# Scoring the next image's first unit ahead of the weighted groups in the middle steps of a vision-tower kernel

## The reference, cut to what matters

```
h  = tokens(x)                              # (16, 256, 192)
q, k, v = split(layernorm(h) @ W_attn + b)  # 12 heads of 16
s  = where(causal, q @ k.T / 4, -inf)       # (16, 12, 256, 256)
h += softmax(s) @ v @ W_proj + b_proj
h += tree_ffn(layernorm(h))
```

## Time and profile before

| | |
|---|---|
| median of 3 runs | 331.52 us (331.21 to 337.34) |
| profiled execution | 332.06 us |
| its span, first to last instruction | 330.3 us |
| PE busy | 267.7 us, 81% |
| VectorE busy | 224.9 us, 68% |
| ScalarE busy | 193.8 us, 59% |
| GpSimd busy | 186.3 us, 56% |
| mean granted TensorE clock | 0.946 of full speed |
| DMA queue of SP and ACT | 23.69 MB in 23,176 packets |

### The profile page before, as it was taken

The page is one execution under the profiler, slowest core; times in us unless marked ns, Lnnn a source line. Parts: engine busy times, 40 slices in busy tenths (PEclk is TensorE's granted clock), DMA queues, the critical chain, the costliest instruction groups (busy, mean ns, idle before and its releaser), DMA issues.

```text
span 330.3 us, 7883 instructions
## 1 busy us (share of the span) xinstructions
PE 267.7 (81%) x2638; PEld 207.2 (63%) x2638; DVE 224.9 (68%) x1126; ACT 193.8 (59%) x393; POOL 186.3 (56%) x322
## 2 busy tenths in 40 slices
PE   0469061187897989999999999999999999999873
PEld 0446051176776667767767767767767777776662
DVE  1054110055488779889888888898898897967872
ACT  2651022045445867867767767768767656858770
POOL 4727777400203567667676676576676575555662
PEclk9997658579999999999999999999999999999997
DMA  4712311001660824625625625624525423000038
GB/s 110 229 35 43 79 22 18 15 0 54 128 108 14 132 78 88 127 89 78 130 78 84 130 79 84 133 75 80 133 83 79 122 85 83 2 5 2 1 98 285
DMA packets 26720, 27.27 MB, mean 83 GB/s; under 512 B 6834, under 2 KB 26416, under 8 KB 26680
## 3 DMA queue, kind: packets, MB, share of 16 engines
q1 hardware_dynamic: 23176, 23.69, 31.7%
q0 software_dynamic: 1568, 2.36, 3.0%
q10 hardware_dynamic: 1936, 0.72, 0.8%
HBM read 4.34 MB, written 3.15 MB: 23 GB/s over the span
## 4 chain that ended last, share of the span: by engine, by line
PE 59%; DVE 10%; POOL 9%; ACT 6%; DMA 6%; issue 6%; SPq 3%; DVEq 0%; ACTq 0%; POOLq 0%
POOL G L342 9%; PE bank L1342 7%; PE bank L1364 7%; PE bank L1308 6%; PE bank L1257 4%; ACT PT L563 4%; PE bank L1279 3%; PE bank L1284 3%; PE bank L1367 3%; DMA G<-x,I 3%; SPq L295 2%; PE bank L1238 2%; PE bank L1304 2%; PE bank L1346 2%; DVE C L846 2%
## 5 line engine op out<-in xcount | busy, mean ns | idle before, releaser
L846 DVE CUSTOM_DVE_ANT_0 C<-bank,MASKV 128x256 bf16<-128x256 f32 (+1 forms) x384 | 112.8, 350 | 19.9 <-PE bank L1308 15.2
L563 ACT ACTIVATE PT<-bank 128x512 f32<-128x512 f32 x144 | 80.8, 598 | 35.0 <-PE bank L1342 30.5
L363 POOL TENSOR_SCALAR_AFFINE_SELECT PT<-PT 128x256 f32<-128x256 f32 x144 | 68.8, 485 | 52.6 <-ACT PT L563 48.6
L347 POOL TENSOR_TENSOR PART<-RES,PART 128x256 bf16<-128x256 f32 (+1 forms) x31 | 28.1, 906 | 25.7 <-ACT PART L557 25.7
L342 POOL DMA_INDIRECT G<-x,I x32 | 30.3, 948 | 15.3 <-issue 9.5
L802 DVE BATCH_NORM_STATS2 ST<-HT 128x6 f32<-128x192 f32 x32 | 9.5, 348 | 32.9 <-ACT HT L515 32.9
L846 DVE DVE_READ_ACCUMULATOR2_ANT MX<- 128x1 f32 x384 | 31.8, 83 | 0.1
L1342 PE MATMUL bank<-QS,KS 98*128 98x256 bf16 x144 | 27.9, 275 | 3.7 <-ACT PT L563 2.6
L1364 PE MATMUL bank<-PT,VA 128*32 128x256 f32 x384 | 30.5, 386 | 0.0
L1308 PE MATMUL bank<-KS,QS 96*128 96x256 bf16 x144 | 27.6, 273 | 1.4 <-DVE MX L846 1.0
L1159 PE MATMUL bank<-ID,G 128*48 128x128 f32 x32 | 6.7, 362 | 23.1 <-DMA G<-x,I 23.1
(11 more groups left out here) (165 smaller groups left out, 649.4 us busy)
## 6 DMA issues: line engine op xcount, KB each, us to landing
QS<-PART SPq DMA_DIRECT2D x72, 96.0 KB, 3.6
KS<-PART SPq DMA_DIRECT2D x72, 96.0 KB, 3.6
out<-HT SPq DMA_DIRECT2D x7, 384.0 KB, 3.6
KSL<-PART SPq DMA_DIRECT2D x24, 96.0 KB, 3.4
QSL<-PART SPq DMA_DIRECT2D x24, 96.0 KB, 3.6
G<-x,I POOLq DMA_INDIRECT x42, 2.5
out<-HT SPq DMA_DIRECT2D x2, 192.0 KB, 3.7
WFS<-wft ACTq DMA_DIRECT2D x2, 144.0 KB, 3.3
```

The source lines that it names most:

```text
L347: pool.tensor_tensor(parts(b)[2][:, ROUNDS[w], :], RES[:, ROUNDS[w], :], parts(b)[1][:, ROUNDS[w], :], ALU.subtract).then_inc(p2_ok, 1)
L363: pool.affine_select(out=e, in_=e, compare_op=ALU.is_ge, fill=0.0, base=0, pattern=[[0, n], [1, P]], channel_multiplier=-1).then_inc(cut_o ...
L563: nc.scalar.activation(PT[:, v, :], BANK[T_BANK[(SU * par + v) % 2]][:, :], ACT.Exp, scale=SCALE).then_inc(exp_ok, 1)
L846: ins = nc.vector.tensor_tensor_reduce(JUNK[:, n:n + keys], bank[:, j * keys:(j + 1) * keys], MASKV[:, S - keys:S], 1.0, LOWEST, ALU.add, ...
```

## The change

Five edits, all for the middle steps, with the closing steps fitted to them:

1. On PE, unit 0 of image b+1 with its wait for the stacking DMAs stands in step b between `project_rest` and the weighted groups, and no longer opens step b+1. Only step 1 still scores its own unit 0. Closing step 14 finds its unit 0 done.
2. On VectorE, the row maximum of that unit stands between the two head evictions.
3. On PE, unit 4 of the scores stands ahead of unit 3 of the transposed scores.
4. On GpSimd, the second piece of the low part stands ahead of the division.
5. The wait for the stacking DMAs is put into a helper, `stack_in`.

```diff
@@ GpSimd, step @@
                 biased(b)
+                if f.off < B:
+                    low(f, 1)
                 if not b.first:
                     normalise(b - 1)
-                if f.off < B:
-                    low(f, 1)
@@ VectorE, step @@
-                row_max(b, par, 0)
+                if b.off == 1:
+                    row_max(b, par, 0)
                 row_max(b, par, 1)
...
                 heads_by_token(d, False)
+                row_max(b + 1, 1 - par, 0)
                 heads_by_token(d, True)
@@ VectorE, closing_step @@
-                row_max(b, par, 0)
+                if not b.late:
+                    row_max(b, par, 0)
@@ TensorE @@
+            def stack_in(b, par):
+
+                for w in range(2):
+                    pe.wait_ge(stacked[w][par], 6 * 16 * (b.off // 2 + 1))
+
             def step(b, par):
...
-                for w in range(2):
-                    pe.wait_ge(stacked[w][par], 6 * 16 * (b.off // 2 + 1))
-                scores(b, par, 0)
+                if b.off == 1:
+                    stack_in(b, par)
+                    scores(b, par, 0)
...
                 scores_t(d, 1 - par, 2)
+                scores(b, par, 4)
                 scores_t(d, 1 - par, 3)
-                scores(b, par, 4)
...
                     project_rest(b - 2)
+                stack_in(b + 1, 1 - par)
+                scores(b + 1, 1 - par, 0)
                 weighted(d, 1 - par, 0)
                 weighted(d, 1 - par, 1)
                 max_t(b)
```

## The result

The changed kernel took 372.23 us (median of 4 runs, 368.57 to 375.54), against 331.37 us for the kernel before in the same rounds: ratio 1.12, 95% interval 1.108 to 1.132. I had forecast 362.4 us, with a range from 352 to 370. The direction and the mechanism were right. The size was not: 40.9 us slower where I had said 30.9. Some executions of most kernels here are some 5 us slower than the others, as a rule by what lies ahead of M(0) (issued at about 109.5 us in them, 105.05 in the trace before) and not in the steps; the ratios leave them out, but for the kernel before in the rounds of experiments 1 to 4, where five of seven executions look like such ones, so that these four ratios may be 1% too low.

A forecast was written before the change was run, and what follows sets the result against it. The chain through M (the row maxima's DMA) bound the kernel before; the change closes a one-step loop, 12.44 + 0.32 + 2.04 = 14.80 us against 12.42. Over 13 steps +30.9: 332.06 + 30.9 = 363.0, median 0.54 lower, 362.4 us; range 352 to 370.

The forecast's parts named there:

- a loop of one step: From one issue of the maxima's DMA through stacking DMAs and PE to the next: 14.80 us against 12.42 before.
- M to unit 0: Loop term from issue of the maxima's DMA to the start of unit 0 of image b+1 on PE: 12.44 us.
- Unit 0 to M: Loop term from unit 0's start on PE to the next issue of the maxima's DMA: 0.32 + 2.04 us.
- the rival: PE's clock falls to 1.2 GHz while it stands at the wait: + 20 on the forecast, 383 us; chance 4%.
- The sum: Thirteen steps, each longer by 14.80 - 12.42 us: +30.9 us.
- The low part ahead of the division: On GpSimd, low part 1.6 us earlier, ending SP's pause among the twelve stacking DMAs: gain only 0.21 us.
- Unit 4 and the row maximum at nothing: PE's moved unit 4 and VectorE's moved row maximum gain only beside the loop of DMAs: nothing for each.
- the first rival: Stacking DMAs land in time after all, so the step shortens by 0.30 us: 328 us; chance 4%.
- the chain through M: In the kernel before, the maxima's DMA takes 2.25 us to land, then transposed scores start; this holds the step.
- the stacking DMAs beside it with nothing to spare: In the kernel before, an image's stacking DMAs land just when its unit 0 is wanted on PE.

The follow-up runs named there:

- experiment 1: Changed kernel with six spare matmuls on PE ahead of the wait for the stacking DMAs in steps 1 to 13: 367.16 us, ratio 1.091.
- experiment 2: Changed kernel with unit 0 and its wait moved behind the transposes of the maxima, ahead of weighted group 2: 334.65 us, ratio 0.997.
- experiment 3: Changed kernel with the maxima's DMA issued by ScalarE right behind its copy, not by SP: 365.19 us, ratio 1.080.
- experiment 4: Changed kernel with the maxima's DMA issued by ScalarE and, on SP, the queries' high-part DMAs moved from tenth place to fourth: 342.86 us, ratio 1.020.
- experiment 6: Changed kernel with two of the twelve stacking DMAs of each image left out from image 4 on: 347.09 us, ratio 1.045.
- experiment 5: Changed kernel with the low part put back behind the division: 389.75 us, ratio 1.162.
- experiment 7: Changed kernel with four of the twelve stacking DMAs of each image left out from image 4 on: 336.4 us, ratio 1.009.
- experiment 8: Kernel before with four of the twelve stacking DMAs of each image left out from image 4 on: 330.96 to 337.62 us, no ratio.
- experiment 10: Kernel before with unit 4 ahead of transposed unit 3, low part ahead of the division, and residual statistics behind the next step's second row maximum: ratio 0.993.
- experiment 11: As experiment 10, with two of the keys' high-part stacking DMAs of images 3 to 15 issued by ScalarE, not SP: ratio 1.007.
- experiment 12: As experiment 11, with ScalarE's two DMAs placed behind the normalisation in the next step's order: ratio 1.012.

## Why the prediction was right and wrong

- **The wait comes too early, and a loop of one step closes.** Right, by the traces and by experiment 2, which opens the loop with everything else in place. Experiment 3 adds what the prediction had not said: two ways lead from M to the stacks, SP's order and ScalarE's order through the low part.
- **M to unit 0, 12.44 us.** Measured 12.56 over thirteen steps, + 1.6 us in all. Image 2 was a good stand-in. That transfers set the pace is right too: 0.83 us for each one left out (experiment 6). The ceiling of 435 GB/s in the Trainium skill ("DMA: Bandwidth & Descriptors", Specifications) does not describe these transfers of one queue: 96 KB in 0.78 us are 126 GB/s.
- **Unit 0 to M, 2.36 us. This is the step that failed**, as the term of the sum that was mis-sized. It is 2.35 us at full clock and 2.82 us on average, 0.46 too little in each of thirteen steps, 6.0 us. I had named the cause as a rival, given it 4%, and put it down by a stretch of step 0 where PE, 77% busy, kept its clock. I misread that stretch. PE's timeline there shows that 3.42 of its 4.26 busy microseconds are ten spare matmuls (L1290, `keep_busy`; two rows each), put there by the kernel before to keep PE at work, and that PE's idle time around them is in pieces of 0.81 and 0.86 us:

```profile
99.38 0.39 PE L1308 MATMUL bank<-KS,QS 96*128 96x256 bf16 x2 [0.81 <-DVE MX L846]
...
100.05 3.42 PE L1290 MATMUL bank<-WP 128*128 128x192 f32 x20
104.33 0.28 PE L1323 MATMUL bank<-IDB,MP 128*24 128x128 bf16 x2 [0.86 <-POOL MP L373]
```

It is a stretch of PE kept at work, as in experiment 1, and not of PE standing in one piece, as here. In the changed kernel the seven waits behind which the clock fell were 2.47 to 3.55 us long, the six others 1.75 to 2.40 us. With 0.62 to 1.44 us it never fell (experiment 6), with 3.08 to 3.87 us always (experiment 5). Between them the length of the wait does not decide alone: in experiment 3 the clock fell behind one wait of 2.14 us and stayed behind another of 2.14, and in step 2 of experiment 6 it fell behind 2.24, less than the 2.40 behind which it stayed in the changed kernel. I had also priced the rival as all or nothing, 383 us; it came in half of the steps, and each time in part of the 2.36 us. The rule of the Trainium skill that I had weighed and set aside ("TensorE: Matmul & The Clock Gate", HAM oscillation) was the better guide, though here seven of thirteen waits brought a fall and not every one.
- **The sum.** In the profiled executions M(0) to M(13) took 161.52 us before and 200.00 us after, + 38.5 of the 39.1 between the two executions, where I had + 30.9: 6.0 more are the clock, 1.6 the transfers. The range was too narrow above for the same reason. It took in the spread of the DMAs, but no part of the clock's; with PE kept at work, in experiment 1, the time of 367.16 us lies in it.
- **The low part ahead of the division, 0.2 us a step.** The pause on SP went, as said, in nine of thirteen steps. The worth was wrong: undone, it costs 1.6 us a step (experiment 5), 0.6 for the later landing and 1.0 for a longer wait and the clock that falls with it.
- **Unit 4 and the row maximum at nothing.** Right behind the stall as far as the traces tell, since both terms of the loop come out without them; no run takes them out of the changed kernel. Without the stall the edits together give what the first rival said and a little more, 0.4 us a step against 0.3 (experiments 7 and 8).
- **What bounds the kernel before.** I had the chain through M as what holds the step, and the stacking DMAs beside it with nothing to spare. Experiment 8 bears out the first: 12.42 us a step with a third of the DMAs gone. The second shows in experiment 10, where PE waits for a late stack as soon as the chain through M is a little shorter.

Open: whether each queue would keep its own rate. Experiment 11 shows only that the last landing came about 1.5 us earlier with two transfers on the other queue, which had a start of 1.15 us, and a version with these behind a wait for M was not run. Open too is what decides whether the clock falls behind a wait of 2.1 to 2.4 us.

## What to carry to other kernels

Before a wait is moved up in an in-order queue, write down everything behind it, and follow each item on until it comes back to what the wait is for. If the path comes back one iteration earlier than before, the wait is no longer hidden by any slack, and its full latency becomes the time of the loop. And when an edit makes PE stand for two microseconds or more in one piece, price the work right behind the wait at both clocks. Before a busy stretch is taken as proof that the clock holds, look at what kept PE busy in it.

## What the runs showed of the hardware

- A 12 KB DMA took 2.1 to 2.3 us to land by itself, and 2.25 to 3.5 us (3.08 on average in experiment 4) when 96 KB transfers that another engine had issued were in flight (experiments 4, 11, 12).
- Back-to-back DMAs of 96 KB from SBUF to SBUF on SP's queue landed 0.78 us apart for image 2 and 0.75 to 0.86 for the others in the traces before and after, while each was issued in 0.62 us.
- ScalarE issued a DMA while the instructions ahead of it in its program were still running (experiment 12, at 197.97). With a wait for the copy's semaphore ahead of it, the DMA went behind the copy (experiment 3, at 191.23).
- Six spare matmuls in the wait, 2.11 us of PE's time, kept the clock at 2.4 GHz and made the kernel faster (experiment 1).
